# Routed experts: VectorE makes the low parts of W1 and W2, weight pieces in three orders, two gate buffers

## The reference, cut to what matters

```python
logits = xn @ Wg + bg
vals, idx = jax.lax.top_k(logits, K)            # K = 2 of E = 8
topk_w = jax.nn.softmax(vals, axis=-1)
def step(acc, params):                          # for each expert
    a = xf @ W1a_e + b1a_e
    b = xf @ W1b_e + b1b_e
    y = jax.nn.silu(a) * b @ W2_e + b2_e
    return (acc + w_e[:, None] * y, None)
...
x = x + gb * _L1_ffn_ref(h, ...)
```

## Time and profile before

| | |
|---|---|
| median of three runs | 2375.85 us |
| the profiled execution, its own time | 2377.58 us |
| its span | 2375.8 us |
| PE busy in the span | 2197.9 us (93%) |
| DVE busy | 1729.6 us (73%) |
| ACT busy | 1329.6 us (56%) |
| Pool busy | 949.3 us (40%) |
| W2 loads (f_raw<-in_W), median from issue to landing | 11.2 us |

### The profile page before, as it was taken

The page is one execution under the profiler, slowest core; times in us unless marked ns, Lnnn a source line. Parts: engine busy times, 40 slices in busy tenths (PEclk is TensorE's granted clock), DMA queues, the critical chain, the costliest instruction groups (busy, mean ns, idle before and its releaser), DMA issues. The chain is left out here.

```text
span 2375.8 us, 38586 instructions
## 1 busy us (share of the span) xinstructions
PE 2197.9 (93%) x12976; PEld 1405.5 (59%) x12976; DVE 1729.6 (73%) x2814; ACT 1329.6 (56%) x2589; POOL 949.3 (40%) x1087
## 2 busy tenths in 40 slices
PE   7978999999999999987999899963999999999998
PEld 5852333333333333326688756643888888888887
DVE  7768787878788787835598868874676667766766
ACT  5533777777677777774344444421555555555554
POOL 4652330313131211202565522455455555554555
PEclk9986999999999999998999999985999999999999
DMA  5669025345261711004000000113454545454542
GB/s 203 163 164 122 1 77 114 77 96 97 78 111 62 144 60 51 11 1 139 26 1 1 9 18 20 52 63 125 145 163 120 160 127 166 120 166 121 168 119 49
DMA packets 126597, 220.46 MB, mean 93 GB/s; under 512 B 16448, under 2 KB 92608, under 8 KB 126016
## 3 DMA queue, kind: packets, MB, share of 16 engines
q1 hardware_dynamic: 104368, 173.28, 21.5%
q0 software_dynamic: 22032, 44.64, 13.7%
HBM read 138.83 MB, written 78.67 MB: 92 GB/s over the span
## 5 line engine op out<-in xcount | busy, mean ns | idle before, releaser
L232 DVE TENSOR_REDUCE tile_max<-p_m 128x2 f32<-128x1024 f32 (+1 forms) x628 | 642.0, 1065 | 134.3 <-PE p_m L224 67.5
L1021 ACT ACTIVATE probs<-p_s 128x512 f32<-128x512 f32 (+3 forms) x1280 | 596.3, 534 | 239.3 <-PE p_s L924 234.0
L2407 PE MATMUL p_up<-f_xT,f_w 128*128 128x512 f32 (+1 forms) x2304 | 473.8, 355 | 25.1 <-POOL f_w L2633 12.7
L864 POOL TENSOR_SCALAR_AFFINE_SELECT probs<-probs 128x128 f32<-128x128 f32 x512 | 145.0, 292 | 694.8 <-ACT probs L1021 685.9
L2407 PEld LDWEIGHTS p_up<-f_xT,f_w 128*128 128x128 f32 x2304 | 369.9, 189 | 86.2 <-issue 26.7
L221 PE MATMUL p_m<-ka,qa 96*128 96x512 bf16 (+1 forms) x1256 | 352.8, 364 | 12.7 <-DVE tile_max L232 5.0
L924 PE MATMUL p_s<-qa,ka 99*128 99x512 bf16 (+3 forms) x1280 | 351.8, 351 | 12.9 <-ACT probs L1021 7.1
L2633 POOL TENSOR_TENSOR f_w<-f_raw,f_w 128x1024 fp32r<-128x1024 f32 x95 | 230.9, 2438 | 277.5 <-ACT f_w L2462 277.5
L938 PE MATMUL p_o<-probs,va 128*32 128x512 f32 (+3 forms) x2560 | 300.3, 541 | 0.6 <-POOL probs L864 0.3
L2422 PE MATMUL p_y<-f_w,f_hidden 128*128 128x256 f32 x1872 | 252.7, 281 | 1.0 <-DVE f_hidden L2560 0.5
L221 PEld LDWEIGHTS p_m<-ka,qa 96*128 96x128 bf16 x1256 | 108.3, 99 | 238.0 <-DVE tile_max L232 135.9
(11 more groups left out here) (292 smaller groups left out, 2748.7 us busy)
## 6 DMA issues: line engine op xcount, KB each, us to landing
x_slots<-mods SPq DMA_DIRECT2D x73, 518.0 KB, 4.2
f_raw<-in_W SPq DMA_DIRECT2D x24, 1024.0 KB, 11.2
f_raw<-in_W1a SPq DMA_DIRECT2D x23, 1024.0 KB, 6.8
f_raw<-in_W1b SPq DMA_DIRECT2D x23, 1024.0 KB, 8.9
qk_scr<-parts SPq DMA_DIRECT2D x48, 256.0 KB, 2.7
qa<-qk_scr POOLq DMA_DIRECT2D x42, 256.0 KB, 15.6
ka<-qk_scr POOLq DMA_DIRECT2D x42, 256.0 KB, 17.3
f_x<-x_slots SPq DMA_DIRECT2D x15, 518.0 KB, 3.7
```

The source lines that it names most:

```text
L232: return nc.vector.tensor_reduce(out=k.tile_max[:, 2 * hp:2 * hp + 2, i, bank], in_=products[:, :, 0:width], op=ALU.max, axis=AX.X)
L864: last = nc.gpsimd.affine_select(block_, block_, pattern=[[1, P]], compare_op=ALU.is_ge, fill=0.0, base=0, channel_multiplier=-1)
L1021: nc.scalar.activation(probs[:, (buf * UNITS + n) % NPROBS, h, lo:CH], p_s[:, s_bank(("exp", HG * n + h), buf), lo:CH], ACT.Exp, scale=DH ...
L2407: last = nc.tensor.matmul(p_up[:, f % 2, ab, 0:size], w1[:, wh, ab * KT + kt, f * P:(f + 1) * P], xT[:, t % 2, xh, kt, 0:size], start=(kt, ...
```

## The change

Pool no longer makes low parts of W1; DVE makes all low parts, of W1 and W2, each behind ACT's rounding of the same piece, in the same step. The single order of the pieces becomes three, chosen by the sizes of a tile and of the tile before it, plus one for the first tile. In each entry the third number is the step: BEFORE + 5 is step 5 of the tile before. Between full tiles it is as before. A half tile behind a full one gets four of its pieces in the full tile (steps 3, 5, 6, 7) and two in its own (0 and 2). A full tile behind a half one gets one piece in the half tile (step 6) and five in its own (two in step 0, then 1, 2 and 3).

In a half tile the weighing of the tile before's y moves from step 2 to step 4 (not in the last tile), ACT's half gate from 4 to 5, the next tile's weights from 4 to 5 and the gate from 5 to 7. The gate gets a second buffer, so that ACT's half gate waits for the weighing of y two tiles back and not of the last one.

```diff
-        y_gate = m.sb("f_y_gate", [P, SPT, D])
+        y_gate = m.sb("f_y_gate", [P, 2, SPT, D])
...
-        pieces = [(1, 0), (2, 0), (1, 1), (1, 2), (1, 3), (2, 1)]
-        PIECES, AHEAD = len(pieces), 3
+        BEFORE, LATE = -FB, -1
+        FROM_START = [(1, 0, LATE), (2, 0, LATE), (1, 1, LATE), (1, 2, 0), (1, 3, 1), (2, 1, 2)]
+        FULL_TO_FULL = [(1, 0, BEFORE + 5), (2, 0, BEFORE + 6), (1, 1, BEFORE + 7), (1, 2, 0), (1, 3, 1), (2, 1, 2)]
+        FULL_TO_HALF = [(1, 0, BEFORE + 3), (1, 1, BEFORE + 5), (2, 0, BEFORE + 6), (1, 2, BEFORE + 7), (1, 3, 0), (2, 1, 2)]
+        HALF_TO_FULL = [(1, 0, BEFORE + 6), (2, 0, 0), (1, 1, 0), (1, 2, 1), (2, 1, 2), (1, 3, 3)]
+        orders = [FROM_START] + [{(ST, ST): FULL_TO_FULL, (ST, HT): FULL_TO_HALF, (HT, ST): HALF_TO_FULL}[two]
+                                 for two in zip(SIZES, SIZES[1:])]
...
-        TURN_AT, AHEAD_AT = 3, FB - AHEAD
-        WEIGH_Y_AT, HALF_GATE_AT, WEIGHTS_AT, GATE_AT = 2, 4, 4, 5
+        TURN_AT = 3
+        WEIGH_Y_AT, HALF_GATE_AT, WEIGHTS_AT, GATE_AT = ({ST: full, HT: half} for full, half in ((2, 4), (4, 5), (4, 5), (5, 7)))
+        LAST_WEIGH_Y_AT = 2
...
+        def pieces_at(t, f):
+            own = [(t, q) for q in range(PIECES) if orders[t][q][2] == f]
+            return own + [(t + 1, q) for q in range(PIECES) if t + 1 < NTILES and orders[t + 1][q][2] == f + BEFORE]
...  (ACT, half_gate_of_y)
-                    if t:
-                        act.wait_ge(y_ready, t)
+                    if t >= 2:
+                        act.wait_ge(y_ready, t - 1)
...  (ACT, end of each step)
-                        if f < PIECES - AHEAD:
-                            round_weights(t, AHEAD + f)
-                        if f >= AHEAD_AT and not last_tile(t):
-                            round_weights(t + 1, f - AHEAD_AT)
+                        for of, q in pieces_at(t, f):
+                            round_weights(of, q)
...  (DVE)
-                def rest_of_w2(t, q):
+                def rest_of_weights(t, q):
                     dve.wait_ge(w_high, PIECES * t + q + 1)
-                    nc.vector.tensor_tensor(piece_part(q, LO), piece_raw(q, t % 2), piece_part(q, HI),
-                                            ALU.subtract).then_inc(w2_ready, 1)
+                    which, n, _ = orders[t][q]
+                    done = w2_ready if which == 2 else w1_ready if (t, n) != (0, 0) else w1_first_ready
+                    nc.vector.tensor_tensor(piece_part(t, q, LO), piece_raw(t, q), piece_part(t, q, HI),
+                                            ALU.subtract).then_inc(done, 1)
...  (DVE, end of each step)
-                        if f < PIECES - AHEAD and pieces[AHEAD + f][0] == 2:
-                            rest_of_w2(t, AHEAD + f)
-                        if f >= AHEAD_AT and not last_tile(t) and pieces[f - AHEAD_AT][0] == 2:
-                            rest_of_w2(t + 1, f - AHEAD_AT)
+                        for of, q in pieces_at(t, f):
+                            rest_of_weights(of, q)
...  (Pool, start of each tile)
-                    for q, (which, n) in enumerate(pieces):
-                        if which == 1 and (t, n) != (0, 0):
-                            pool.wait_ge(w_high, PIECES * t + q + 1)
-                            nc.gpsimd.tensor_tensor(piece_part(q, LO), piece_raw(q, t % 2), piece_part(q, HI),
-                                                    ALU.subtract).then_inc(w1_ready, 1)
```

More of the change, by code:

```diff
@@ L2298, in routed_experts, with piece @@
         blocks_to = [sum(SIZES[:t]) // P for t in range(NTILES + 1)]
-        pieces = [(1, 0), (2, 0), (1, 1), (1, 2), (1, 3), (2, 1)]
-        PIECES, AHEAD = len(pieces), 3
+        BEFORE, LATE = -FB, -1
[5 more added lines that the diff above has]
+                                 for two in zip(SIZES, SIZES[1:])]
+        PIECES = len(FROM_START)
         F1P, F2P = 2, FB // 2
         PIECES1, PIECES2 = FB // F1P, FB // F2P
-        TURN_AT, AHEAD_AT = 3, FB - AHEAD
-        WEIGH_Y_AT, HALF_GATE_AT, WEIGHTS_AT, GATE_AT = 2, 4, 4, 5
+        TURN_AT = 3
+        WEIGH_Y_AT, HALF_GATE_AT, WEIGHTS_AT, GATE_AT = ({ST: full, HT: half} for full, half in ((2, 4), (4, 5), (4, 5), (5, 7)))
+        LAST_WEIGH_Y_AT = 2
         WEIGHT_OWN = 5
-        def piece(q, one, two):
-            which, n = pieces[q]
+        def pieces_at(t, f):
+            own = [(t, q) for q in range(PIECES) if orders[t][q][2] == f]
+            return own + [(t + 1, q) for q in range(PIECES) if t + 1 < NTILES and orders[t + 1][q][2] == f + BEFORE]
+        def piece(t, q, one, two):
+            which, n, _ = orders[t][q]
             if which == 1:
@@ L2314, in piece, with piece_raw, piece_part @@
             return two[:, n * F2P:(n + 1) * F2P, :]
-        def piece_raw(q, par):
-            return piece(q, raw1[:, par, :, :], raw2[:, par, :, :])
-        def piece_part(q, part):
-            return piece(q, w1[:, part, :, :], w2[:, part, :, :])
+        def piece_raw(t, q):
+            return piece(t, q, raw1[:, t % 2, :, :], raw2[:, t % 2, :, :])
+        def piece_part(t, q, part):
+            return piece(t, q, w1[:, part, :, :], w2[:, part, :, :])
         def last_tile(t):
@@ L2448, in round_weights @@
                 def round_weights(t, q):
-                    (which, n), par = pieces[q], t % 2
+                    (which, n, _), par = orders[t][q], t % 2
                     if which == 1:
@@ L2540, in gate_of_y @@
                         dve.wait_ge(half_gated, blocks_to[t] + u + 1)
[L2541 to L2542 removed]
+                        row = y_gate[:, t % 2, u, :]
+                        last = nc.vector.scalar_tensor_tensor(out=row, in0=k.mods[1][:, 1, GB, :],
+                                                              scalar=batch_weight[:, t % 2, 1, u:u + 1], in1=row,
                                                               op0=ALU.mult, op1=ALU.add)
                     last.then_inc(gate_ready_y, 1)
[L2546 removed]
+                def rest_of_weights(t, q):
                     dve.wait_ge(w_high, PIECES * t + q + 1)
[L2548 to L2549 removed]
+                    which, n, _ = orders[t][q]
+                    done = w2_ready if which == 2 else w1_ready if (t, n) != (0, 0) else w1_first_ready
+                    nc.vector.tensor_tensor(piece_part(t, q, LO), piece_raw(t, q), piece_part(t, q, HI),
+                                            ALU.subtract).then_inc(done, 1)
                 def hide(t, f):
@@ L2562, in hide @@
                                             ALU.subtract).then_inc(hidden_ready, 1)
-                    if f == WEIGH_Y_AT and t:
+                    if f == (LAST_WEIGH_Y_AT if last_tile(t) else WEIGH_Y_AT[size]) and t:
                         weigh_y(t - 1)
@@ L2578, in weigh_y @@
                     rows = y[:, t % 2, 0:blocks, :]
-                    nc.vector.tensor_tensor(rows, rows, y_gate[:, 0:blocks, :], ALU.mult).then_inc(y_ready, 1)
+                    nc.vector.tensor_tensor(rows, rows, y_gate[:, t % 2, 0:blocks, :], ALU.mult).then_inc(y_ready, 1)
                 rest_of_x(0)
-                dve.wait_ge(w_high, 1)
-                nc.vector.tensor_tensor(piece_part(0, LO), piece_raw(0, 0), piece_part(0, HI), ALU.subtract).then_inc(w1_first_ready, 1)
-                rest_of_w2(0, 1)
+                for t, q in pieces_at(0, LATE):
+                    rest_of_weights(t, q)
                 find_rows(0)
```

16 lines of the change are left out of this document (7 added, 9 removed).

## The result

The changed kernel took 2395.51 us (median of four runs, 2394.89 to 2396.88) against 2376.7 for the kernel before (four runs, 2372.61 to 2378.04): ratio 1.008, 95% interval 1.0067 to 1.0092. It is slower, by 18.8 us; the forecast was slower by 6, and the range ended at 2389. The profiled execution took 2395.5 us, its span is 2393.8.

A forecast was written before the change was run, and what follows sets the result against it. Half tiles stay bound by ACT and DVE, not PE. Eight half-full pairs at +0.89 give +7.1, the last half tile -0.8: +6.3 us, median 2382 (bounds 2378 to 2386); 8-in-10 range 2371 to 2389.

The forecast's parts named there:

- The chain of the half tile: Half tile (H, 256 tokens) after full tile (F, 512): ACT and DVE links sum to 23.41 us, 0.72 won.
- H5: Step 5 of the half tile, where the next tile's weights are made: 2.40 us, as before.
- The F after H: Full tile behind a half one: third up group starts 8.62 us after the first, against 7.10 before.
- The term 1.61: Full tile behind a half one: 1.52 us lost before its third up group plus 0.09 for a second cold restart.
- up group 3.04 (cold): First up group of a full tile behind a half one: 3.04 us on PE, taken from the earlier rows.
- 0.02 a link: Error allowed for hand-overs and overlaps in some 25 links: a pair moves by 0.5, the sum by 4 us.
- at the low clock: First tile: three up groups run without a gap at the low clock, second quarter in time; no change.
- half tiles at PE's pace: Rival: at the eight half tiles DVE keeps up and PE never waits; 33 us won, 2343; chance 4%.
- the weak form of that rival: Only the wait at the full tile's third up group doesn't form; -6.6 us, 2369; chance 12%.
- the balance of waits: Rival: the full tile's new wait is half the forecast, the half tile's gain stands; no change, 2376; chance 17%.
- The rival that what stays on Pool stops DVE: Pool's small exponential at full-tile steps 5 and 6 stops DVE 0.75 us per half tile; +6 more, 2388; chance 12%.
- The nine-piece F tiles: Rival: full tiles between two half ones (6, 14, 22) fall behind, 3 x 2 us more, 2388; chance 5%.

The follow-up runs named there:

- e1: Changed kernel with quarter 1 of W1 ahead of half 0 of W2 in full tiles behind half ones; 2385.67 us, ratio 1.0036 to the kernel before.
- e2: Changed kernel plus 16 unread PE transposes before the first up group of each full tile behind a half one; 2386.87 us, ratio 1.0039 to the kernel before.
- e8: Changed kernel plus five unread PE transposes before each half tile's first down group; 2393.04 us, ratio 1.007 to the kernel before.
- e10: Changed kernel with the old single order and steps, plus 95 128x1024 scratch subtractions on Pool that nobody waits for; 2428.72 us, ratio 1.022 to the kernel before.

## Why the prediction was wrong in size, point by point

- **The chain of the half tile** held. Forecast from the end of up group 7 of the full tile: 4.28, 3.06, 1.88, 3.06, 3.08, 2.43, 2.40, 3.22, in sum 23.41. Measured from the gates above (1724.95 + 2.96 = 1727.91; 1732.21, 1735.27, 1737.13, 1740.18, 1743.27, 1745.71, 1748.34, 1751.57): 4.30, 3.06, 1.86, 3.05, 3.09, 2.44, 2.63, 3.23, in sum 23.66. Only H5 is off, by 0.23: the sum of the exponentials (L2534) took 0.46 there, and 0.23 at its old place. Pool's scatter of y runs beside it in both kernels. Order of time, changed kernel, then before:

```profile
1746.55 1.58 POOL L2622 DMA_INDIRECT out<-f_y,f_y_to  x1 [20.51 <-issue]
```

```profile
1744.92 1.55 POOL L2612 DMA_INDIRECT out<-f_y,f_y_to  x1 [0.30 <-issue]
...
1745.72 0.23 DVE L2524 TENSOR_SCALAR f_exp_sum<-f_gap_exp 128x4 f32<-128x4 f32 x1
```

The sum began 0.60 into the scatter and ended 1.06 into it; before, it began 0.80 in and ended 1.03 in. It is so in all eight half tiles of both kernels within 0.02, while it takes 0.16 where no scatter runs. It looks as if it were held until about 1.05 into a scatter. That follows from the times alone: no run moved the scatter to test it, and once (1960.78), 0.58 into a longer scatter of 1.95, the sum took 0.16. Won per half tile: 0.47, not 0.72.
- **The F after H**: first to third up group forecast 8.62, measured 8.65. The term 1.61 measured 1.56 + 0.10. e1 shows its cause: with the two pieces swapped 1.13 of it goes.
- **The sum of these two** is 1.2 a pair (H to H 90.09 before, 91.31 after, where no group is slow), not 0.89: 1.22 x 8 = 9.8 us for eight pairs instead of 7.1.
- **The step that failed** is "up group 3.04 (cold)". I took the price of the F's first up group from the earlier trace rows, where PE had waited 1.58, and used it behind a wait that I had myself put at 2.3. There the clock fell to its lower level in five of eight groups, 4.58 instead of 3.03, and PE's next start came 1.54 later: 7.7 us. e2 takes the idle time away with all else kept and these 8 to 9 us go; e8 covers another wait and four of eight groups are still slow. No range of mine held this term: I had written that no row shows PE's restart in these places, and then allowed 0.02 a link for it. The nearest row told nothing of what a longer wait does. This is the largest part of the miss; the chain of ACT and DVE, which was the work of the prediction, was right to 0.3 us a pair, and slower was the right side.
- **The start of the stage and the last half tile**: tile 2 started 0.85 later, at 1729.15 and not 1728.30. All of it stands before the pattern: the stage's first up groups started at 1661.30 (1660.74 before), which arises ahead of the changed part and is of the size by which executions differ (between 1657.8 and 1663.0 in the twelve profiles), and the first 36 matmuls took 10.70 instead of 10.41. The prediction has these "at the low clock"; the granted clock was 0.81 over them before and 0.79 after, so only the first part of them was on the lower level, and 0.3 us hangs on when it rises. The last tile took 29.84 from its first up group to the end of the span, 30.33 before: -0.5, forecast -0.8.
- Together 9.8 + 7.7 + 0.85 - 0.5 = 17.9 of the 18.0 us between the spans.
- **Nothing elsewhere**: full tiles before an H (1.67 for the gate's four operations, forecast 1.7) and full tiles after full ones (34.03) came as forecast.

The rivals: half tiles at PE's pace needed 20.5 us of chain and got 23.66. The third up group's wait formed in full, so neither the weak form of that rival nor the balance of waits held. The rival that what stays on Pool stops DVE put it on Pool's exponential, at 0.75 a half tile. For the exponential the order of time refutes it, changed kernel:

```profile
1723.86 2.18 POOL L2632 TENSOR_TENSOR f_gap_exp<-f_euler,f_x 128x4 f32<-128x4 f32 x1 [4.91 <-DMA f_x<-x_slots]
1723.91 1.22 DVE L2561 TENSOR_TENSOR f_w<-f_raw,f_w 128x1024 fp32r<-128x1024 f32 x1
```

DVE's low part took its usual 1.22 inside Pool's 2.18; it is Pool's exponential that is stretched (1.04 in the earlier trace rows). The Trainium skill (GPSIMD Engine Reference, section Key points) says that GpSimd contends with DVE instructions with two SBUF inputs; the traces agree for 128x1024 operations on Pool (2.91 instead of 1.22 in e10), while this one of 128x4 cost DVE nothing. What seems to cost it something is the scatter, by the rows above: 0.23 a half tile, 1.8 of the 9.8 us that the pairs lost. The nine-piece F tiles did not fall behind either: H to H with such a tile only was 58.37 (55.59 before), and 55.59 + 1.22 + 1.54 is 58.35.
